# The median's last search moves into the back transform of an attention block

## The reference

```
q_in = quantile(x.reshape(B, C, -1), 0.5)          # lower/upper median mean, per channel
x = x + relu(-q_in)
y = upfirdn2d(x, lpf, up=2); y = max(y, 0); y = upfirdn2d(y, lpf, down=2)
spec = rfft2(y); gate = sigmoid(fg_w2 @ gelu(fg_w1 @ |spec|))
xf = y + irfft2(spec * gate)
q = xf_flat @ q_w + q_b
k1, v1 = kv_path(xf, 8x8 convolution, stride 8);  k2, v2 = kv_path(xf, 16x16 convolution, stride 16)
out = softmax(q k^T / 4) v @ proj_w + proj_b + y    # 4 heads, 256 + 64 keys, 16384 queries
```

## Time and profile before

| | |
|---|---|
| median of three runs | 12782.41 us |
| profiled execution | 12788.18 us, span 12786.9 us |
| mean granted PE clock | 0.889 |
| PE busy | 10858.8 us, 85% |
| DVE busy | 8881.2 us, 69% |
| ACT busy | 7243.7 us, 57% |
| POOL busy | 2643.0 us, 21% |
| first inverse matmul to first maxima, ninth pass | 142.23 us |

### The profile page before, as it was taken

The page is one execution under the profiler, slowest core; times in us unless marked ns, Lnnn a source line. Parts: engine busy times, 40 slices in busy tenths (PEclk is TensorE's granted clock), DMA queues, the critical chain, the costliest instruction groups (busy, mean ns, idle before and its releaser), DMA issues. The chain is left out here.

```text
span 12786.9 us, 196006 instructions
## 1 busy us (share of the span) xinstructions
PE 10858.8 (85%) x71137; PEld 5608.2 (44%) x71137; DVE 8881.2 (69%) x15501; ACT 7243.7 (57%) x12109; POOL 2643.0 (21%) x4368
## 2 busy tenths in 40 slices
PE   2898897988979888798888989889898897988979
PEld 1534435344353543535344353443534435344353
DVE  6677676776667767667676677766677676776766
ACT  5556464664646646466464655646566464664646
POOL 1212212122131221212222121221212212122130
PEclk9899898988979889798897989979898897988979
DMA  1021220202212021130211202112021221202213
GB/s 45 18 50 35 43 58 25 56 21 47 54 27 53 28 45 50 30 70 15 42 46 36 64 18 43 42 41 60 18 53 32 44 57 26 55 21 49 52 28 66
DMA packets 168920, 531.33 MB, mean 42 GB/s; under 512 B 64008, under 2 KB 86536, under 8 KB 153168
## 3 DMA queue, kind: packets, MB, share of 16 engines
q1 hardware_dynamic: 168016, 518.95, 18.1%
HBM read 230.33 MB, written 67.11 MB: 23 GB/s over the span
## 5 line engine op out<-in xcount | busy, mean ns | idle before, releaser
L943 DVE TENSOR_REDUCE R<-ps 128x2 f32<-128x640 f32 x4096 | 3194.9, 818 | 919.0 <-PE ps L680 908.9
L1148 ACT ACTIVATE R<-ps 128x512 f32<-128x512 f32 x5120 | 2820.8, 594 | 645.8 <-PE ps L701 620.3
L246 ACT ACTIVATE R<-R,st 128x1475 bf16<-128x1475 f32 x1326 | 2018.2, 1522 | 852.9 <-DVE st L312 756.9
L300 DVE TENSOR_SCALAR_CACHE_REDUCE R<-R,st 128x1255 bf16<-128x1255 f32 x1326 | 2011.6, 1517 | 20.8
L680 PE MATMUL ps<-KST,R 96*128 96x320 bf16 x8192 | 1879.8, 313 | 64.7 <-DVE R L943 54.5
L726 PE MATMUL ps<-R 128*32 128x512 f32 x12288 | 1634.4, 605 | 37.9 <-DVE Wk L894 32.8
L701 PE MATMUL ps<-R,KST 104*128 104x512 bf16 x4096 | 1578.3, 388 | 21.3 <-ACT R L1148 20.6
L680 PEld LDWEIGHTS ps<-KST,R 96*128 96x128 bf16 x8192 | 763.2, 100 | 827.3 <-DVE R L943 303.7
L1232 POOL CAST R<-Wk 128x512 bf16<-128x512 f32 x256 | 283.4, 1107 | 2625.0 <-DVE Wk L894 2625.0
L701 PEld LDWEIGHTS ps<-R,KST 104*128 104x128 bf16 x4096 | 396.4, 97 | 708.4 <-ACT R L1148 460.1
L463 PE MATMUL ps<-R,cst 64*128 64x512 f32 x2048 | 584.7, 646 | 128.7 <-ACT R L1041 93.6
(11 more groups left out here) (206 smaller groups left out, 20064.1 us busy)
## 6 DMA issues: line engine op xcount, KB each, us to landing
R<-R SPq DMA_DIRECT2D x3072, 64.0 KB, 2.4
R<-xh_in SPq DMA_DIRECT2D x136, 512.0 KB, 4.3
out_dram<-Z SPq DMA_DIRECT2D x16, 4096.0 KB, 13.2
R<-xa_in SPq DMA_DIRECT2D x36, 1024.0 KB, 11.4
R<-xb_in SPq DMA_DIRECT2D x34, 1024.0 KB, 17.9
R<-sr_in SPq DMA_DIRECT2D x32, 1024.0 KB, 4.8
R<-sr_in SPq DMA_DIRECT2D x16, 2016.0 KB, 8.4
R<-sr_in SPq DMA_DIRECT2D x16, 1056.0 KB
```

What stands on the lines that cost most here:

```text
L246: e.activation(junka[:, 0:o2 - o1], xc[:, o1:o2], ACT.Sign, bias=mid, scale=-1.0, accum_out=cnt[:, NP + i:NP + i + 1]).then_inc(md_ca, 1)
L300: e.tensor_scalar(junk[:, 0:o1 - o0], xc[:, o0:o1], mid, None, ALU.is_le, ALU.add, accum_out=cnt[:, i:i + 1]).then_inc(md_cv, 1)
L943: e.tensor_reduce(MX[(4 * u + s4) % 2][:, blk_, h0:h0 + 2], ps[:, 2 + 2 * bq:4 + 2 * bq, 0:320], axis=AX.X, op=ALU.max).then_inc(mx, 1)
L1148: e.activation(PB[:, t % 2, w, :], ps[:, w % 2, :], ACT.Exp).then_inc(ex, 1)
```

## The change

The 16 rounds of the last search are called from inside the 18 rounds of the back transform. On DVE one `slot` stands behind the product with the gate (L873) and one behind the addition that makes XF (L878). On PE `slot(2)` stands at the end of each round, and two extra `yield`s ahead of the rounds make PE sum each mask one round later than it otherwise would. MF has three buffers, so that a mask waits for the mask three rounds earlier, and MF and TF move from Wk to R5, where the bisection's unused output stood. Slots in the transposes and in the second convolution are gone. The tail on PE is called at taps 2, 5 and 8 of the first convolution, on DVE between the copies of the transposes and the first query block. SP no longer waits for `md_v` ahead of the last transfer of taps.

```diff
-        MF = [W[:, 256 * i:256 * i + 256].bitcast(BF16) for i in range(2)]
-        TF = [W[:, 512 + 512 * i:1024 + 512 * i] for i in range(2)]
+        MF = [R5[:, 256 * i:256 * i + 256].bitcast(BF16) for i in range(3)]
+        TF = [R5[:, 768 + 512 * i:1280 + 512 * i] for i in range(2)]
...
# pe_median, ahead of the 16 rounds
+            for _ in range(2):
+                yield
             for i in range(17):
...
# dve_median
-                    if i > 1:
-                        e.wait_ge(md_tb, i - 1)
-                        e.wait_ge(md_fs, i - 1)
-                    e.tensor_scalar(MF[i % 2], xc[:, 512 * i:512 * i + 512], hi, BIG, ALU.is_le, ALU.mult).then_inc(md_ta, 1)
+                    if i > 2:
+                        e.wait_ge(md_tb, i - 2)
+                        e.wait_ge(md_fs, i - 2)
+                    e.tensor_scalar(MF[i % 3], xc[:, 512 * i:512 * i + 512], hi, BIG, ALU.is_le, ALU.mult).then_inc(md_ta, 1)
...
# tensor: back transform, transposes, convolutions
                     e.matmul(ps[:, 2 + k, :], lhsT=c("edft"), rhs=RR[k], start=True, stop=True).then_inc(xi_ps, 1)
+                slot(2 if n < 17 else 1)
...
                 op.then_inc(xt_ps, 1)
-                slot(1)
...
                               rhs=XFT[:, j::4, i::8], start=n < 2, stop=n >= 30)
+                slot(1 if n in (2, 5, 8) else 0)
             op.then_inc(c1_ps, 1)
-            slot(4)
+            for _ in med:
+                pass
             for j in range(1, 4):
                 stage(0, j, 6)
                 conv2(j - 1)
-                slot(4)
             conv2(3)
-            for _ in med:
-                pass
...
# vector: back transform, copies of the transposes, query blocks
                                     ALU.mult).then_inc(av, 1)
+                slot(1 if n < 17 else 0)
...
                                     ALU.add).then_inc(xf, 1)
+                slot(1 if n < 16 else 0)
...
                               ps[:, grp % 4, :].rearrange("p (v h) -> p v h", h=S)).then_inc(xfd, 1)
-                slot(2)
+            for _ in med:
+                pass
...
                 e.tensor_tensor(zj, zj, c("pb").unsqueeze(2).to_broadcast([128, C, 32]), ALU.add).then_inc(zb, 1)
-                slot(4)
-            for _ in med:
-                pass
...
# sync
-            e.wait_ge(md_v, STEPS + 2)
             e.dma_start(TAP2[:, 65:128, :], sr2w[:, 65:128, :]).then_inc(in_w2[2], 16)
```

More of the change, by code:

```diff
@@ L211, in pe_median @@
                         j = q % 2
-                        op = e.matmul(ps[64 * j:64 * j + 64, 7, 336:464], lhsT=pairb[:, :], rhs=MF[i % 2][:, 128 * q:128 * q + 128],
+                        op = e.matmul(ps[64 * j:64 * j + 64, 7, 336:464], lhsT=pairb[:, :], rhs=MF[i % 3][:, 128 * q:128 * q + 128],
                                       start=i == 0 and q < 2, stop=i == 15 and q > 1)
@@ L269, in pool_median @@
                         e.wait_ge(md_mm, i - 1)
-                    e.tensor_tensor(TF[i % 2], MF[i % 2], xc[:, 512 * i:512 * i + 512], ALU.add).then_inc(md_tb, 1)
+                    e.tensor_tensor(TF[i % 2], MF[i % 3], xc[:, 512 * i:512 * i + 512], ALU.add).then_inc(md_tb, 1)
                 yield
@@ L1222, in gpsimd @@
             slot(18)
-            slot(16)
+            for _ in med:
+                pass
             def stage(g, j, bk):
```

## The result

The changed kernel took 12385.19 us (median of four runs, 12365.55 to 12394.99), the kernel before on the same chip 12784.62. The ratio is 0.9683, 95% interval 0.9672 to 0.9695. The forecast was 12390. The profiled execution of the changed kernel is its fastest run, 12365.55 us; the one of before took 12788.18.

What follows compares the result with a forecast made beforehand. PE paces the back transform while DVE waits; in the transposes PE waits for DVE. Terms summed to -25.25 us a pass (short ones -23.35), -394.6 in all: 12788.18 to 12393.6, forecast 12390 for a median, range 12345 to 12508.

Steps and rivals of the forecast that it cites:

- Start, +1.2: Start of the back transform: PE's last count precedes the first inverse matmul, which starts 1.2 us later a pass.
- Rounds, +3.2: Back transform: four mask matmuls on PE add 0.2 us to each of 16 rounds, +3.2 us a pass.
- Transposes, -18.6: Transposes: 64 in a row at full clock, 27.25 us becomes 8.6, so -18.6 us a pass.
- 0.5 us put aside for a fall of the clock: Transposes: 0.5 us added for a clock fall after the 1.1 us wait for the last piece of XF.
- First convolution, +1.3: First convolution with the tail inside: first wait 0.73 us, three small matmuls 0.2 each, later waits covered; +1.3 us a pass.
- Second convolution and end, -6.75 and -4.05: Second convolution 18.06 us in place of 24.81; after its last tap 0.5 in place of 4.55.
- Chain to the keys, -0.6: Chain to the keys: full clock for one matmul, 0.7 us in place of 1.33, so -0.6 us a pass.
- Half clock in the transposes: Rival: transposes fall to half clock, 14.9 us in place of 8.6; +116 us, 12506; chance 0.1.
- DVE and POOL: Rival: they hold each other up in the back transform, 3.7 us a round, not 3.15; +141 us, 12531; chance 0.1.
- The transfers: Rival: query tiles land 3.2 us after the keys in each pass, cover being 1.8 us; +51 us, 12441; chance 0.04.
- serial chain: Slower rival: each back-transform round becomes one chain of 7.0 us; 13370 us in all; chance 0.03.
- The short passes: Five of sixteen passes, 3.3 us shorter before the change, were to gain 23.35 us each, 1.9 less than the others.

Runs made afterwards that it cites:

- the even variant: Changed kernel with the tail called behind taps 3, 7 and 11 of the first convolution, not 2, 5 and 8: 12377.31 us, ratio 0.9681.
- the last group: Four variants of the changed kernel run together (no lag; tail behind second convolution; more DVE work; idle PE): 12748.01, 12429.08, 12492.44, 12574.9 us.

## Why the prediction was right

**What bounded the kernel.** Right. In the back transform PE sets the pace and DVE waits; in the transposes and behind the convolutions it was the reverse. Moving the search gained 18.9 us a pass in the transposes and 6.75 behind the first convolution, and cost 1.0 in the back transform. That the lag was needed for it is shown by the run without it, and that DVE had room by the run with more work. SP's wait, which the change also takes away, was not tried alone; neither profile has a wait of PE for a transfer in the second convolution of the ninth pass.

**Start, +1.2.** It measured +1.60. The wait for ACT's last count was right (PE's count starts at 6593.83, 0.09 us behind ACT); two pairs of matmuls at half clock took 0.92 and not 0.6.

**Rounds, +3.2.** The whole back transform measured +1.02. A round grew by 0.09 us, half of the 0.17 read from the row of eight masks: 0.14 us pass from the first mask to the next inverse matmul, and from there to the next L597 it is 1.84 us, where it was 1.90 (6841.64 to 6843.54) before. In the ninth pass the full clock also returned 3.9 us behind the first inverse matmul, 5.5 before.

**Transposes, -18.6.** Measured -18.91, at a clock of 1.00 all through. The 0.5 us put aside for a fall of the clock was not needed. The weighing of the Trainium skill's rule against the first pass's row came out on the row's side; the run with an idle PE shows it apart.

**First convolution, +1.3: the mis-sized term.** It measured +3.66. The step that failed is "the later waits of the tail lie behind three taps of about 0.46 us each". A tap is not 0.46 us: two taps, which write different halves, run together in 0.92, and one left alone takes as long. Three taps take as long as four. Four odd groups (3, 3, 3, 23) lose 4 x 0.46 = 1.84 us, and the even variant gave just 1.85 back; the rest is the first wait and the small matmuls.

**Second convolution and end, -6.75 and -4.05.** Both came out to 0.01 us, since the windows before held the same matmuls at the same clock.

**Chain to the keys, -0.6.** Measured -1.40: the full clock lasts for three matmuls, 0.58 us each, and not for one. In three of 16 passes the chain took 16.93 and not 16.35.

**The rivals.** Half clock in the transposes did not come. DVE and POOL do meet in each round, but POOL is the one held up (1.55 us for 1.16), DVE's product keeps its time, and PE does not wait. The transfers stayed hidden by 1.4 us, 1.8 reckoned: SP began at 6689.85, the last of the first unit's 24 landed at 6706.93, and the first maxima at 6708.37 were released by ACT. With the lag there is no serial chain; without it a milder form came, 4.56 us a round.

**The short passes.** They are gone. Before, the full clock came back 2.7 to 2.9 us behind the first inverse matmul in those five and 5.1 to 5.8 in the others. They held the same work and took 3.0 us less in the mean: 1.3 in the back transform, 1.1 in the transposes, the rest behind. After the change it is 3.5 to 4.7 in all sixteen, and their stretches differ by 1.2 us at most.

The ninth pass measured -27.0 us from the last sigmoid on (143.42 to 116.41), against -25.25. By the table's means the back transform (2.2 less than reckoned) and the chain (0.8 less) made up for the convolution (2.4 more) and the start (0.4 more). So the sum is nearer than its terms are, and that is luck. The profiled execution, 12365.55, lies 28 us under the sum's 12393.6; the median lies 5 under the forecast, which is nearer than such a sum can be trusted to be. The prediction's 117 us for the whole stretch is the old 142.23 less the whole gain, the start's loss counted in; counted so, the ninth pass took 115.2 (142.23 - 27.0).

## What to carry to other kernels

Put side work of one engine into the stage in which another engine sets the pace, and read the room from that stage's idle time a round: 0.47 us there was right to 0.1, as the run with more work showed. Where the producer stands behind its own wait for PE, let its consumer on PE come one round later; without that lag the two engines took turns here. Before cutting into a run of matmuls, look whether they go in pairs, and cut only between pairs.

## What had not been expected of the hardware

The taps of the first convolution (float32, 64 columns of weights, 256 columns moved), which write different halves of PSUM's partitions in turn, run two at a time, and one alone takes as long as two: three taps and the start of the next matmul 1.97 us, four taps 1.97.

Single runs spread more than the four first ones of each kernel show: 13 runs of the kernel before beside the last group went from 12762.49 to 12801.39. Between the profiles of kernels whose edits do not touch these stages, the filters take 176.4 to 178.2 us a pass in the mean with 32.2 to 36.7 us at half clock, and the attention 352.4 to 353.9 with 23.7 to 28.1. The longer ones are those with more half clock. A gain of under 1 us a pass is thus lost in where the clock falls, and the even variant's 2 us nearly are. The runs point the same way: of the eight without the lag the two slowest have a mean granted clock of 0.908 and the two fastest 0.910. That the clock is the cause of the spread between runs is argued from this, not shown.
